# Four cross-attention layers on one core: score pairs on two row groups in the 32-head layer, V split from PSUM and turned blocks in twos in the 16-head layers

## The reference, cut to what matters

```
x = L0(x, ctx)            # one head
x = L1(x, ctx, mask)      # 32 query heads of 16, 8 key/value heads of 16, then layer norm
x = L2(x, ctx, ctx)       # norm, attention (16 heads of 128), norm, attention again, norm, MLP
x = L3(ctx, x, mask)      # 16 heads of 32, norm, MLP

# L1:  q = x@Wq+bq ; k,v = ctx@Wk+bk, ctx@Wv+bv
#      attn = softmax(q k^T / 4 + mask) ; y = attn v ; out = norm(y@Wo + bo + x)
# L2:  k,v get one more row (bias_k, bias_v); out = x + softmax(q k^T / sqrt(128)) v @ wo + bo
```

## Time and profile before

| | us |
|---|---|
| median of 3 runs (lowest, highest) | 4720.5 (4711.0, 4727.8) |
| the profiled execution | 4721.1 |
| its span | 4719.3 |
| PE, DVE, ACT, POOL busy | 4137.2, 2761.8, 2005.7, 1078.6 |

### The profile page before, as it was taken

The page is one execution under the profiler, slowest core; times in us unless marked ns, Lnnn a source line. Parts: engine busy times, 40 slices in busy tenths (PEclk is TensorE's granted clock), DMA queues, the critical chain, the costliest instruction groups (busy, mean ns, idle before and its releaser), DMA issues.

```text
span 4719.3 us, 59734 instructions
## 1 busy us (share of the span) xinstructions
PE 4137.2 (88%) x21554; PEld 3102.2 (66%) x21554; DVE 2761.8 (59%) x4220; ACT 2005.7 (42%) x3484; POOL 1078.6 (23%) x996
## 2 busy tenths in 40 slices
PE   6799699997999987897887996999979999878978
PEld 5555388886888865544664554888868888655446
DVE  2377666566666554666424785666565665546664
ACT  2377444333444332564223773344333343225542
POOL 1421223223133223000214212133132232230002
PEclk9899799998999988998987997999989999888989
DMA  1210111011011011000212001011010110210002
GB/s 64 56 19 10 36 34 41 21 36 41 25 41 39 19 54 49 9 2 10 69 64 56 19 10 45 25 41 36 21 41 25 41 41 16 62 41 9 2 11 70
DMA packets 151667, 159.44 MB, mean 34 GB/s; under 512 B 14022, under 2 KB 118667, under 8 KB 151443
## 3 DMA queue, kind: packets, MB, share of 16 engines
q1 hardware_dynamic: 143762, 146.96, 10.3%
q0 software_dynamic: 7680, 9.45, 1.2%
HBM read 144.84 MB, written 2.10 MB: 31 GB/s over the span
## 4 chain that ended last, share of the span: by engine, by line
PE 62%; DVE 15%; issue 9%; ACT 8%; POOL 3%; DVEq 1%; DMA 1%; POOLq 0%; SPq 0%; ACTq 0%
PE ps L146 15%; PE ps L148 14%; PE ps L147 14%; PE ps L1722 3%; DVE w_v_lo L1846 3%; PE ps L1335 3%; PE ps L904 2%; DVE w_mx L1835 2%; ACT w_p L1780 2%; PE ps L1323 2%; PE ps L886 2%; PE ps L916 2%; PE ps L1347 2%; ACT w_v_hi L1772 1%; DVE w_pt_lo L1851 1%
## 5 line engine op out<-in xcount | busy, mean ns | idle before, releaser
L1851 DVE TENSOR_TENSOR w_pt_lo<-ps,w_pt_hi 128x512 fp32r<-128x512 f32 x512 | 351.5, 687 | 195.5 <-ACT w_pt_hi L1787 195.5
L1787 ACT ACTIVATE w_pt_hi<-ps 128x512 fp32r<-128x512 f32 x512 | 298.3, 596 | 336.8 <-PE ps L1722 335.8
L1460 DVE CUSTOM_DVE_ANT_0 g_units<-ps,g_mask 128x1024 f32<-128x1024 f32 x256 | 312.2, 1219 | 143.9 <-PE ps L1323 102.6
L1722 PE MATMUL ps<-ident,w_p 128*128 128x128 f32 x2048 | 315.4, 280 | 71.1 <-DVE w_pt_lo L1851 71.1
L1722 PEld LDWEIGHTS ps<-ident,w_p 128*128 128x128 f32 x2048 | 255.6, 144 | 149.9 <-DVE w_pt_lo L1851 95.4
L1835 DVE TENSOR_REDUCE w_mx<-ps 128x1 f32<-128x1024 f32 x256 | 311.5, 1217 | 50.2 <-PE ps L148 50.2
L1643 POOL CAST w_wo_hi<-w_raw 128x1024 fp32r<-128x1024 f32 x32 | 35.1, 1096 | 1283.0 <-PE ps L148 1283.0
L1407 ACT ACTIVATE g_units<-g_units,g_nmx 128x1024 f32<-128x1024 f32 x256 | 294.4, 1150 | 54.8 <-DVE g_nmx L1460 52.0
L1778 ACT ACTIVATE w_ex<-w_xl,w_nm 128x1 f32<-128x1 f32 x256 | 75.5, 295 | 552.8 <-DVE w_nm L1841 552.8
L1335 PEld LDWEIGHTS ps<-ident,g_units 128*128 128x128 f32 x2048 | 227.9, 145 | 110.8 <-issue 66.9
L1335 PE MATMUL ps<-ident,g_units 128*128 128x128 f32 x2048 | 292.9, 287 | 7.8 <-ACT g_turned L1415 5.9
(11 more groups left out here) (363 smaller groups left out, 10863.7 us busy)
## 6 DMA issues: line engine op xcount, KB each, us to landing
w_raw<-in_L_xattn_wk SPq DMA_DIRECT2D x32, 512.0 KB, 3.5
w_raw<-in_L_xattn_wq SPq DMA_DIRECT2D x32, 512.0 KB, 3.6
w_raw<-in_L_xattn_wv SPq DMA_DIRECT2D x32, 512.0 KB, 3.6
w_raw<-in_L_xattn_wo SPq DMA_DIRECT2D x32, 512.0 KB, 3.6
mlp_raw<-in_L_xattn_w_fc SPq DMA_DIRECT2D x64, 256.0 KB, 2.8
mlp_raw<-in_L_xattn_mlp_w SPq DMA_DIRECT2D x64, 256.0 KB, 2.8
ctx_nat<-in_ctx SPq DMA_DIRECT2D x4, 1024.0 KB, 13.0
g_mask<-in_mask_Bx1xSxS_ff SPq DMA_DIRECT2D x2, 2048.0 KB, 9.6
```

What stands on the lines that cost most here:

```text
L1460: dve.tensor_tensor_reduce(units[:, q % U, :].rearrange("p (h w) -> p h w", h=2), ps[:, 2 * (q % 2):2 * (q % 2) + 2, :], mask[:, q % 4, :] ...
L1722: i = pe.transpose(ps[:, T_BANK + tn % 2, lt * P:(lt + 1) * P], prob[:, u, lt, v * P:(v + 1) * P], ident[:, :])
L1787: act.activation(pt.h[:, x[2] % 4, :], ps[:, T_BANK + tn % 2, :], ACT.Copy).then_inc(t_hi, 1)
L1851: dve.tensor_tensor(pt.l[:, x[2] % 4, :], ps[:, T_BANK + tn % 2, :], as_f32(pt.h[:, x[2] % 4, :]), ALU.subtract).then_inc(t_free, 1)
```

## The change

In `grouped()`: the two matmuls of a score pair use different partitions of the array (0 to 47 for the first half of the keys, 64 to 111 for the second), so `qs` holds each head's queries twice and `ks` one half of the keys in each place. The transfers are made by `spread_k` and `spread_q`, six each, in an order in which a few go ahead of the first score and the rest behind it; `qs` is held once. POOL splits the weights first and clears afterwards, PE makes Q before V, and DVE clamps the mask. In `wide()`: V's bias is added in place in PSUM, the high and low parts are made from the bank, two of the four V steps stand at a chunk's start, and turned blocks are made in twos.

```diff
-            qs = sb(own, tag + "_qs", [P, 2, 4, NQ], F32R)
-            ks = sb(own, tag + "_ks", [P, C, NK], F32R)
+            qs = sb(own, tag + "_qs", [P, HEADS, NQ], F32R)
+            ks = sb(own, tag + "_ks", [P, KV, NK // 2], F32R)
...
+            def spread_k(pool, kv, ready):
+                for h in range(2):
+                    for blk, src in enumerate((kd.h, kd.l, kd.h)):
+                        at_ = 64 * h + DH * blk
+                        pool.dma_start(ks[at_:at_ + DH, kv, :],
+                                       src[kv * DH:(kv + 1) * DH, h * 512:(h + 1) * 512]).then_inc(ready, 16)
+            def spread_q(pool, u, ready):
+                for h in range(2):
+                    for blk, src in enumerate((qd.h, qd.h, qd.l)):
+                        at_ = 64 * h + DH * blk
+                        pool.dma_start(qs[at_:at_ + DH, u, :], src[u * DH:(u + 1) * DH, :]).then_inc(ready, 16)
...
             def pool_(pool, b):
+                split_kv(pool, wk, raw_k)
+                split_q(pool, b, 0)
+                split_kv(pool, wv, raw_v)
                 pool.memset(vd[:, :, :, :], 0.0)
...
+                spread_k(pool, 0, first_ready)
+                pool.wait_ge(kq_done, b * KQ + 3)
+                spread_q(pool, 0, first_ready)
+                for u in range(1, 4):
+                    spread_q(pool, u, qs_ready[0])
+                spread_k(pool, 1, ks_ready[0])
+                for u in range(4, HEADS):
+                    spread_q(pool, u, qs_ready[1])
+                split_q(pool, b, 1)
+                for kv in range(2, KV):
+                    spread_k(pool, kv, ks_ready[1])
+                split_o(pool, b, 0)
+                for c in range(1, C):
...
+                    pool.wait_ge(s_full, b * STEPS + c * 32 - 16)
+                    for u in range(4):
+                        spread_q(pool, u, qs_ready[0])
+                    spread_rz(pool, g)
+                    pool.wait_ge(s_full, b * STEPS + c * 32)
+                    for u in range(4, HEADS):
+                        spread_q(pool, u, qs_ready[1])
...
+                        elif q == 4:
+                            pe.wait_ge(qs_ready[0], (b * 15 + 3) * 6 * 16)
...
-                        p0 = 64 * (u // 4)
                         for h in range(2):
+                            p0 = 64 * h
                             i = pe.matmul(ps[:, 2 * (q % 2) + h, :],
-                                          qs[p0:p0 + 3 * DH, c % 2, u % 4, i_ * P:(i_ + 1) * P],
-                                          ks[p0:p0 + 3 * DH, c, h * 512:(h + 1) * 512],
+                                          qs[p0:p0 + 3 * DH, u, i_ * P:(i_ + 1) * P],
+                                          ks[p0:p0 + 3 * DH, 2 * c + u // 4, :],
...
                 dve_q(dve, b, 0)
+                dve.wait_ge(loaded["m"], b * 16 + 16)
+                for lt in range(LT):
+                    dve.tensor_scalar(mask[:, lt, :], mask[:, lt, :], -1.0e38, None, ALU.max)
...
             order = lines("""
-                k.0.0 k.0.1 q.0 k.1.0 x.0
+                k.0.0 k.0.1 q.0 v.0 vh.0 vl.0 k.1.0 v.1 vh.1 vl.1 x.0
...
                 elif key[0] == "v":
-                    eng.wait_ge(v_sum, (r * C + c) * 4 + key[1] + 1)
+                    eng.wait_ge(v_done, (r * C + c) * 4 + key[1] + 1)
...
-                        act.activation(vv.h[:, 2 * x[1]:2 * x[1] + 2, :], v32[:, x[1] % 2, :, :],
+                        act.activation(vv.h[:, 2 * x[1]:2 * x[1] + 2, :],
+                                       bank(c, ("v", x[1])).rearrange("p (q w) -> p q w", q=2),
...
-                        dve.tensor_tensor(v32[:, x[1] % 2, :, :], bank(c, x).rearrange("p (q w) -> p q w", q=2),
+                        dve.tensor_tensor(both, both,
...
-                        dve.tensor_tensor(vv.l[:, 2 * i:2 * i + 2, :], v32[:, i % 2, :, :],
+                        dve.tensor_tensor(vv.l[:, 2 * i:2 * i + 2, :],
+                                          bank(c, ("v", i)).rearrange("p (q w) -> p q w", q=2),
```

More of the change, by code:

```diff
@@ L1143, in grouped @@
             first = ExitStack()
-            kd, vt = Pair(first, tag + "_k", [P, NK]), sb(first, tag + "_vt", [P, NK])
+            vt = sb(first, tag + "_vt", [P, NK])
             raw_k, raw_v = (sb(first, tag + "_raw_" + x, [P, KC, P]) for x in "kv")
@@ L1247, in pool_ @@
-                split_q(pool, b, 0)
-                pool.wait_ge(kq_done, b * KQ + 2)
[L1249 to L1253, removed]
-                for c in range(C):
+                pool.wait_ge(kq_done, b * KQ + 2)
@@ L1262, in pool_ @@
-                    if c == 0:
-                        pool.wait_ge(loaded["m"], b * 16 + 16)
-                        for lt in range(LT):
-                            pool.tensor_scalar(mask[:, lt, :], mask[:, lt, :], -1.0e38, None,
-                                               ALU.max).then_inc(mask_ready, 1)
+                    pool.wait_ge(s_full, b * STEPS + c * 32 - 16)
+                    for u in range(4):
+                        spread_q(pool, u, qs_ready[0])
+                    spread_rz(pool, g)
@@ L1290, in pe_q, with pe_kv @@
                     i.then_inc(ring_full, 1)
-            def pe_(pe, b):
-                for n, w in ((0, wk), (1, wv)):
-                    pe.wait_ge(split["kv"], b * 2 + n + 1)
-                    for h in range(2):
-                        for k in range(KC):
-                            i = mm3(pe, ps[:, 2 * n + h, :], w[:, k, :], CT[:, k, h * 512:(h + 1) * 512],
-                                    k == 0, k == KC - 1)
-                        i.then_inc(pre_full, 1)
+            def pe_kv(pe, b, n, w):
+                pe.wait_ge(split["kv"], b * 2 + n + 1)
+                for h in range(2):
+                    for k in range(KC):
+                        i = mm3(pe, ps[:, 2 * n + h, :], w[:, k, :], CT[:, k, h * 512:(h + 1) * 512],
+                                k == 0, k == KC - 1)
+                    i.then_inc(pre_full, 1)
+            def pe_(pe, b):
+                pe_kv(pe, b, 0, wk)
                 pe.wait_ge(split["q"], b * C + 1)
@@ L1302, in pe_ @@
                 pe_q(pe, b, 0, range(KC))
+                pe_kv(pe, b, 1, wv)
                 for h in range(2):
@@ L1389, in act_ @@
                                    bias=cols[:, c_bk:c_bk + 1]).then_inc(kq_hi, 1)
+                act_q(act, b, 0)
                 for h in range(2):
@@ L1827, in dve_ @@
                         dve.wait_ge(cv_done, g + 1)
-                        dve.tensor_tensor(v32[:, x[1] % 2, :, :], bank(c, x).rearrange("p (q w) -> p q w", q=2),
+                        both = bank(c, x).rearrange("p (q w) -> p q w", q=2)
+                        dve.tensor_tensor(both, both,
                                           cv[:, :].unsqueeze(1).broadcast_to([P, 2, 256]),
```

91 lines of the change are left out of this document (44 added, 47 removed).

## The result

The changed kernel takes 4586.75 us (median of 4 runs, 4583.06 to 4594.86) against 4715.75 us (4710.94 to 4727.77) of the kernel before on the same chip: a ratio of 0.9725, 95% interval 0.970 to 0.975. The profiled execution's span is 4587.5 us, 131.8 less than before.

The account below looks back on a forecast made before the run. PE was taken as pacing the steady 32-head stretch, after POOL's transfers delayed its start, and as idle 2.66 us per 16-head chunk. Gains 37 + 20 + 32 = 89 us gave 4721 - 89 = 4632 us, range 4580 to 4678.

Parts of the forecast that it names:

- Part 1: Start of the 32-head stage: earlier first score and product with V, 18.3 us a batch element, 37 us for both.
- slower than 0.49 us while DVE clamps: 32-head start: sign that the early-start forecast is wrong, if POOL issues transfers slower than this during DVE's mask clamps.
- steps 4 to 8: 32-head start: all taken at 1.2 GHz, 2.84 us each, putting the product with V at 199.8 us.
- upper end of 51 us: 32-head start: largest gain, if the clock stays up through the five steps, some 1.7 us each instead of 2.84.
- Part 2: 32-head score pairs on different rows: second matmul starts 0.11 us earlier, 0.33 us per four steps, 20 us.
- fully side by side: Rival, 32-head score pairs: row groups overlap completely, 22 us more gain, 4610 us; chance 0.10.
- an estimate of 42 us: 32-head score pairs: gain by the skill's 4 ns between starts, 3 x 0.236 x 59.5, not used in the sum.
- The count of three pairs in four: 32-head steady stretch: three of four pairs' savings reach the end, 0.33 us for four steps.
- Part 3: 16-head chunks: shorter low part of V and new order cut PE's wait by 1.0 us a chunk, 32 us.
- The walk: 16-head chunk: counting PE's and DVE's work from the last V step, 1.4 us of 2.4 us waiting remain.
- The wait only moved: Rival, 16-head chunks: the new order merely shifts its wait and gains 0, 4664 us; chance 0.15.
- Half clock in the steady stretch: Rival, 32-head stage: pairs leave PE at 1.2 GHz, 6.8 us more per four steps, 4834 with half; chance 0.04.

Follow-up runs that it names:

- 32-head half alone: Changed kernel's 32-head code with the 16-head layers of the kernel before: 4635.55 us, ratio 0.983 to the kernel before.
- 16-head half alone: Changed kernel's 16-head code with the 32-head layer of the kernel before: 4674.03 us, ratio 0.991 to the kernel before.
- pairs on the same rows: Changed kernel with both matmuls of a score pair on partitions 0 to 47: 4633.58 us, 46.8 us over the changed kernel.
- all transfers first: Changed kernel, but a 32-head stage's first score waits for all 60 transfers of its first chunk instead of 12: 4628.98 us.

## Why the prediction was right, and where its sizes were off

The time, 4586.75 us, is faster as forecast and in the range, 45 us below the value of 4632. By the spans 42.8 us are missing from the sum of 89: 25.2 in the 32-head stages, 13.5 in the 16-head attentions, 4.1 elsewhere.

- **Part 1 (37 us): right in place and size.** With the row groups taken out the two stages are 758.4 - 722.5 = 35.9 us shorter than before, and the product with V comes 48.4 us after the start instead of 65.6. From the stage's start the first score stands at 24.4 us and step 4 at 33.1, both as forecast, the score by two misses of 0.6 us that cancel: the first transfer was issued 16.4 us after the start where I had 17.0, and the first six took 3.65 us where I had 3.1. My sign "slower than 0.49 us while DVE clamps" came true with that, at 0.61. The clock was off: two of the steps 4 to 8 ran at half of it, not all five, so the product with V came at 42.8 us instead of 47.4. The upper end of 51 us comes out as 48 by its own terms (37 + 10 x 1.14).
- **Part 2 (20 us): the mechanism was right and the price of a pair too small.** It was sized by "I read loads as one after the other even when they go to different places, at 0.10 us a load of 128 columns", so 0.11 us a pair. Measured are 0.23 us a pair and 46.3 us in all, 35.1 in the steady stretches and 11.2 ahead of the first products with V, where the clock came back sooner, which I hadn't foreseen: the rival "fully side by side" came true, and a pair is worth twice what I gave it. The eight loads of the earlier trace rows led me wrong: they go to column groups of the same rows, and tell nothing of two row groups. The Trainium skill, TensorE: Matmul & The Clock Gate, section "🔬 Part 3: Packing small matmuls — row/col tiling", has a spacing of some 4 ns, from which I had worked out an estimate of 42 us. The trace agrees on the spacing, 3 ns in the median. The count of three pairs in four was near: 17.7 us in the first stage over 29.75 fours of steps are 0.60 us a four, 2.6 pairs of 0.23.
- **Part 3 (32 us): the wait was right, its company was not.** The walk left 1.4 us of 2.4 and the trace shows 1.24; the waits fell from 71.1 to 39.7 us, 31.4 in all. Of the other 14 us, 11.7 are PE's own work: it is busy 2316.9 us in the four attentions instead of 2328.6, and this is mostly the clock. Of before's chunks some took 69 us:

```profile
885.00:890.00 5.00, 2.60 (x15) 1.65 (x13) 4.18 (x7) 2.88 (x6) 3.42 (x2) 0.98 0.25 92
890.00:895.00 5.00, 4.99 (x22) 4.30 (x23) 2.17 (x5) 1.72 (x3) 0.00 (x0) 0.67 0.31 101
...
875.25:944.43 69.18, 66.52 (x370) 56.54 (x370) 41.77 (x64) 27.65 (x52) 18.47 (x12) 0.98 0.12 35
```

```profile
890.01 1.12 PE L1722 MATMUL ps<-ident,w_p 128*128 128x128 f32 x4 [2.00 <-DVE w_pt_lo L1851]
```

After the pauses of 0.4 and 2.0 us PE works at half clock for some us, and the chunk is 1.5 us longer (the last window is one whole chunk, with PE busy 66.52 us instead of 65.01). The pauses don't do it every time: the chunk of the earlier trace rows has the same two, and its clock stayed at 1.00. The kernel before has 13 such drops in the chunks of its four attentions, and so has the 32-head half alone; the changed kernel, the 16-head half alone and the old order with V split from PSUM have none. At 1.5 us each they come to 20, of which a chunk's PE work that is 0.2 us longer in the new order (65.2 against 65.0) takes back 6. No stretch of the changed kernel's first attention between 560 and 1060 us is below 1.00. I priced the wait and not what it did to the clock. And I put the gain down to V's low part and the order together, where each would have done much of it alone: 60.2 us for the split from PSUM, 33.8 for the order, 45.5 for both in the profiled runs. On top of the split the order cost 11 us.
- **The rivals.** "The wait only moved" is out (71.1 to 39.7 us). Half clock in the steady stretch is out (1.00 from 193 to 480 us).

## What to carry to other kernels

Price two matmuls on different row groups as one, and look next at the engines that were hidden behind them. Where DVE subtracts two on-chip operands, see what POOL does at that time: reading PSUM, or another place for the step, gave back 0.6 us each on average here and 2.0 at most. Change a list of steps and a data path apart from each other: here the path alone was worth 60 us, the list alone 34 and the two together 46, while two moves read from the two waits that the old list had left gave 34 more.

## What was unexpected of the hardware

After PE had idled, the low clock lasted differently by what PE did then. With score pairs on one row group (before, and "pairs on the same rows", two stages each) it held past the first product with V, until 26 to 32 us after the first score, though PE was busy 5.00 of 5 us for the last 10 of them and more. With pairs on two row groups it was back by the first product with V in every stage, 21 us after the first score at the latest (without the clamps on DVE), and 8 and 10 us after it in the two stages of "all transfers first". Why, no run here settles.
